# Attention kernel: the context copied out of its bank by ScalarE, the inverted row sums spread into their own bank, and new hand-written orders

## The reference

```python
qn  = layer_norm(x, q_norm_g, q_norm_b);  kvn = layer_norm(context, kv_norm_g, kv_norm_b)
Q, K, V = heads(qn @ Wq), heads(kvn @ Wk), heads(kvn @ Wv)
attn = softmax(Q @ K.T / sqrt(32))
ctx  = merge_heads(attn @ V)
out  = x + gelu(ctx @ Wo + bo)            # exact gelu
```

## Time and profile before

| what | value |
|---|---|
| median of 2 runs | 3285.81 us (3284.95 to 3286.67) |
| profiled execution, its own time | 3289.35 us |
| its span | 3287.5 us |
| PE busy | 3251.8 us, 99% of the span |
| DVE, ACT, POOL busy | 2255.8, 2278.0, 2314.0 us (69, 69, 70%) |
| DMA engines | about 60% busy |
| TensorE clock granted, mean | 0.995 |

### The profile page before, as it was taken

One profiled execution on the slowest core, in us unless ns is written; L12 is line 12 of the kernel. 1 busy time (PEld: TensorE's weight loads), 2 busy tenths in 40 slices (PEclk: granted clock), 3 DMA queues, 4 the chain that ended last, 5 costly groups with the idle time before them and its releaser, 6 DMA issues.

```text
span 3287.5 us, 60427 instructions
## 1 busy us (share of the span) xinstructions
PE 3251.8 (99%) x16611; PEld 2140.6 (65%) x16611; DVE 2255.8 (69%) x4775; ACT 2278.0 (69%) x3986; POOL 2314.0 (70%) x1543
## 2 busy tenths in 40 slices
PE   8999999999999999999999999999999999999998
PEld 5566666666666666666666666666666666666664
DVE  6677676776676676667766766766677667667664
ACT  4677767776667777677667667776776676677765
POOL 2677677777767776776777677767767766777765
PEclk9999999999999999999999999999999999999999
DMA  6566556566566666565665566665656655666653
GB/s 141 76 111 106 104 103 115 90 108 109 104 107 96 109 104 105 103 117 86 109 108 105 105 97 109 106 103 103 120 83 111 106 105 105 99 110 107 102 77 74
DMA packets 186492, 340.15 MB, mean 103 GB/s; under 512 B 20561, under 2 KB 20577, under 8 KB 186466
## 3 DMA queue, kind: packets, MB, share of 16 engines
q1 hardware_dynamic: 186000, 339.03, 60.0%
q10 hardware_dynamic: 466, 0.80, 0.2%
HBM read 104.87 MB, written 33.55 MB: 42 GB/s over the span
## 4 chain that ended last, share of the span: by engine, by line
PE 97%; DVE 1%; issue 1%; ACT 1%; DMA 0%; POOL 0%; SPq 0%; ACTq 0%; POOLq 0%; DVEq 0%
PE gen L820 42%; PE score L847 15%; PE score L840 15%; PE ctx L864 14%; PE gen L876 4%; PE gen L910 4%; PE gen L930 1%; DVE maxes L684 0%; POOL probs L463 0%; DMA k_stack<-k_nat 0%; PE score L766 0%; ACT q_stack L598 0%; PE ctx L795 0%; DVE stats L703 0%; PE gen L809 0%
## 5 line engine op out<-in xcount | busy, mean ns | idle before, releaser
L463 POOL TENSOR_TENSOR probs<-probs 128x1024 f32<-128x1024 f32 x762 | 1803.0, 2397 | 290.6 <-PE ctx L864 284.6
L684 DVE TENSOR_REDUCE maxes<-score 128x1 f32<-128x512 f32 x2048 | 1295.3, 681 | 199.9 <-PE score L847 199.0
L546 ACT ACTIVATE probs<-score 128x512 f32<-128x512 f32 x2048 | 1086.3, 620 | 141.3 <-PE score L840 136.2
L847 PE MATMUL score<-k_stack,q_stack 96*128 96x512 f32 x2048 | 761.2, 413 | 3.2 <-DVE maxes L684 2.2
L840 PE MATMUL score<-q_stack,k_stack 128*128 128x512 f32 x2048 | 698.1, 407 | 6.4 <-ACT q_stack L598 6.3
L847 PEld LDWEIGHTS score<-k_stack,q_stack 96*128 96x128 f32 x2048 | 378.5, 189 | 217.1 <-ACT probs L546 82.9
L840 PEld LDWEIGHTS score<-q_stack,k_stack 128*128 128x128 f32 x2048 | 374.1, 189 | 202.4 <-DVE maxes L684 58.2
L864 PE MATMUL ctx<-probs,v_sb 128*32 128x512 f32 x4096 | 492.5, 598 | 1.1 <-DVE ctx_n L700 1.1
L820 PE MATMUL gen<-w_v,cT 128*128 128x512 f32 x1536 | 462.2, 395 | 0.0
L820 PE MATMUL gen<-cT,w_k 128*128 128x512 f32 x1536 | 460.0, 398 | 0.2 <-DVE q_nat L666 0.2
L820 PE MATMUL gen<-xT,w_q 128*128 128x512 f32 x1536 | 450.5, 396 | 3.4 <-DVE w_q L622 0.4
(11 more groups left out here) (88 smaller groups left out, 2748.2 us busy)
## 6 DMA issues: line engine op xcount, KB each, us to landing
k_stack<-k_nat SPq DMA_DIRECT2D x384, 256.0 KB, 8.4
q_stack<-q_nat SPq DMA_DIRECT2D x381, 256.0 KB, 5.6
tok<-in_x SPq DMA_DIRECT2D x132, 256.0 KB, 10.4
tok<-in_ctx SPq DMA_DIRECT2D x128, 256.0 KB, 11.0
res<-in_x SPq DMA_DIRECT2D x124, 256.0 KB, 2.7
out<-res SPq DMA_DIRECT2D x124, 256.0 KB, 2.1
probs<-in_L_xattn_Wq SPq DMA_DIRECT2D x1, 1024.0 KB, 7.6
probs<-in_L_xattn_Wk SPq DMA_DIRECT2D x1, 1024.0 KB, 9.9
```

Of the source, the lines that this page charges most:

```text
L463: pool.tensor_tensor(probs[:, c + 1, heads], probs[:, c + 1, heads], probs[:, c, heads], ALU.add).then_inc(pool_added, 1)
L546: act.activation(probs[:, n, part, :], score_at(s, "st", i)[:], ACT.Exp, scale=SCALE).then_inc(exp_done, 1)
L684: dve.tensor_reduce(maxes[:, u1 % 2, SROW + i:SROW + i + 1], score_at(s, "s", i)[:], AX_X, ALU.max, negate=True).then_inc(max_done, 1)
L847: pe.matmul(score_bank(pe, b, s, "s", i)[:, :], q_stack[0:KROWS, u1 % 2, n, P * part:P * (part + 1)], k_stack[0:KROWS, u1 % 2, n, :], star ...
```

## The change

ACT gets a new instruction in each step, `cc`: it copies `ctx_ps` to a new tile `ctx_raw` in SBUF once the second `pv` is done, and it is now this copy that raises `ctx_read`. DVE's `zb` writes the spread inverses to the gen bank from which `zt` read the sums, instead of to `ctx_n`; `cn` multiplies `ctx_raw` by that bank and it is now `cn` that releases the gen bank (`free["z"]`). The space for `ctx_raw` comes from smaller tiles (`ones` has 32 columns, `max_hl` shares `max_cut`, some constants share a tile, the norm rows are loaded into `max_cut` before the first batch). The order of all five engines is new; the number of items of each kind over a batch is the same, apart from `cc`.

```diff
 OVER_BATCH = ("v", "o", "gelu", "res_add", "store", "res", "load", "ln", "la", "lv", "norm", "x", "first_res", "ob")
 ORDER = {
     "pe": (
-        "q*3 v q*2 v q v st*2 v*2 s st v s st s v*2 st s st s z v st*3 s v*2 st*2 s st k v s*4 pv st s st*2 o s "
-        "st s k s*2 pv m k o*2 k o k*2",
-        "o st*2 o st*3 q st q*4 st q st*3 z x k*3 x st*2 x st k*2 s k st s st*2 pv s x s x s x s pv s x s*2 o*3 "
-        "s*2 x o s o*2 s o s o*2 s o s o*3 m",
-        "o*4 s o s k s k s st k s st z st s st s q st q st s st*2 k st*3 k s st k st*4 pv s*2 q s q s*2 q s*2 q "
-        "pv m",
-        "k q k v q v k*2 st*3 k st*2 q st*2 k q st q st q st*2 z st*4 v st v s*3 pv s*2 v s*2 v s*2 v s v s*2 v*2 "
-        "s*2 v s*2 v pv m",
+        "q*3 v q*2 v q v st v st*3 v*2 s v s st*2 v s st*2 v z s k s st k s pv st v s st v s*2 v st s st k s st s "
+        "st*2 s*4 pv m o*3 k*3",
+        "o*2 st*2 o st*3 q st q st*3 q*2 st q*2 st x z st k*6 s x st x st*3 pv s x s x s x s*3 pv x o*2 s x o s o "
+        "s o s*2 o*4 s*2 o s*2 o*4 m",
+        "o*2 s*2 k o*2 k s*3 st k s q st k s q st*2 s st k st*4 z st*2 s*2 q st*3 k s st*2 pv s*2 q s*2 q*2 s pv "
+        "m",
+        "k q*2 k q k v k st*2 v st k st*2 q k st v st q st*3 q st*2 z st s st v st s st s pv s*3 v*2 s v s*2 v "
+        "s*2 v s*2 v s v*2 s*2 pv m",
     ),
     "act": (
-        "q st*4 v st*8 norm v split norm*2 st*4 mh mx*4 k",
-        "st*6 gelu q st x st*2 norm st*4 x k st*2 norm x norm st x*2 norm x norm x*2 gelu mh gelu mx*4 split",
-        "gelu st*12 k split st*4 q mh mx*4",
-        "st*6 k st*5 q st*4 split st v*2 mh mx*4",
+        "q st*2 cc st*2 v st*4 norm st norm*2 st split st v st*5 mh mx*4 k",
+        "st*8 gelu q cc x st*2 norm st*2 norm x k st x st*2 norm st x norm*2 x*4 gelu mh gelu mx*4 split",
+        "gelu st*2 cc st*11 k st*3 q mh split mx*4",
+        "st cc st*4 k st*5 q st*6 v split v mh mx*4",
     ),
     "dve": (
-        "q s ln s*2 la ln lv s ln s la*2 zt s zr lv zb s cn ln lv s la s*3 lv s*5 md ml ln*2 k ob",
-        "ln la*2 q zt lv*2 x la zr ln zb cn lv s la x k lv s x s*2 x*2 s*2 x s*3 x s*2 x s ob s*4 md ob ml",
-        "s ob s*6 zt s zr zb cn s k s*7 md q ml",
-        "k zt zr zb cn q s*16 md ml",
+        "q ln s*2 ln s la ln la lv*2 la ln s zt ln lv zr s zb cn la s*2 la s*3 lv s*6 md ml ln k ob",
+        "la ln la lv*2 q x zt zr ln zb cn lv s x la k x lv s*4 x*2 s x s x s*2 x s*2 ob s*5 md ob ml",
+        "s*2 ob s*6 zt zr s*2 k s zb cn s*5 md q ml",
+        "k zt s zr q s zb s cn s*13 md ml",
     ),
     "pool": (
-        "ln*3 split add*6 res_add ln*3",
-        "ln*2 add*5 res_add add res_add split res_add",
-        "split add*6",
+        "ln*3 add ln split add*5 res_add ln",
+        "ln*3 add*4 res_add add res_add add split",
+        "res_add add*6 split",
         "add split add*5",
     ),
     "sp": (
-        "load*8 rq rk store res",
-        "rq rk store res store",
-        "store first_res rk rq first_res",
+        "load*8 rq rk store",
         "rq rk",
+        "res store res store*2 rk rq first_res",
+        "first_res rq rk",
     ),
 }
 
...
+        ctx_raw = sb("ctx_raw", [P, D])
...
-        ones = sb("ones", [P, P])
+        ones = sb("ones", [P, DH])
...
+                        if kind == "cc" and valid(bp):
+                            wait(act, pv_done, 4 * (NU * bp + up) + 4)
+                            wait(act, free["z"], NU * bp + up)
+                            act.activation(ctx_raw[:], ctx_ps[:], ACT.Identity).then_inc(ctx_read, 1)
                         if kind == "split" and valid(bp):
-                            wait(act, ctx_read, NU * bp + up + 1)
+                            wait(act, free["z"], NU * bp + up + 1)
...
                             wait(dve, full["z"], tp + 1)
                             wait(dve, ctx_split, tp)
-                            dve.transpose(ctx_n[:], gen_at("z", up)[:]).then_inc(free["z"], 1)
+                            dve.transpose(ctx_n[:], gen_at("z", up)[:]).then_inc(z_turned, 1)
                         if kind == "zr" and valid(bp):
-                            wait(dve, free["z"], tp + 1)
+                            wait(dve, z_turned, tp + 1)
                             dve.reciprocal(z_inv[:], ctx_n[:].rearrange("p (b c) -> p b c", c=DH)[:, :, 0]).then_inc(z_inverted, 1)
                         if kind == "zb" and valid(bp):
                             wait(dve, z_inverted, tp + 1)
-                            dve.transpose(ctx_n[:].rearrange("p (b c) -> p b c", c=DH),
+                            dve.transpose(gen_at("z", up)[:].rearrange("p (b c) -> p b c", c=DH),
                                           z_inv[:].unsqueeze(2).to_broadcast([P, NZ, DH])).then_inc(z_spread, 1)
                         if kind == "cn" and valid(bp):
                             wait(dve, z_spread, tp + 1)
-                            wait(dve, pv_done, 4 * tp + 4)
-                            dve.tensor_tensor(ctx_n[:], ctx_ps[:], ctx_n[:], ALU.mult).then_inc(ctx_read, 1)
+                            wait(dve, ctx_read, tp + 1)
+                            dve.tensor_tensor(ctx_n[:], ctx_raw[:], gen_at("z", up)[:], ALU.mult).then_inc(free["z"], 1)
```

More of the change, by code:

```diff
@@ L201, in build @@
         ident = sb("ident", [P, P])
-        ones = sb("ones", [P, P])
+        ones = sb("ones", [P, DH])
         maxes = sb("maxes", [P, 2, P])
         max_cut = sb("max_cut", [P, P], F32R)
-        max_hl = sb("max_hl", [P, P], F32R)
-        cut_sign = sb("cut_sign", [P, 1])
-        low_row = sb("low_row", [P, 1])
+        row_consts = sb("row_consts", [P, 3])
+        cut_sign, low_row, minus_half = (row_consts[:, n:n + 1] for n in range(3))
         chunk_mask = sb("chunk_mask", [P, NC])
@@ L216, in build @@
         rstd = sb("rstd", [P, 8])
-        minus_half = sb("minus_half", [P, 1])
-        bias_q = sb("bias_q", [P, NU])
-        bias_k = sb("bias_k", [P, NU])
-        bias_v = sb("bias_v", [P, NU])
-        norm_rows = sb("norm_rows", [4 * NC, P])
+        bias_qkv = sb("bias_qkv", [P, 3, NU])
+        bias_q, bias_k, bias_v = (bias_qkv[:, n, :] for n in range(3))
         norm_cols = sb("norm_cols", [P, 4, NC])
@@ L652, in prepare @@
                     dve.wait_ge(bias_mm, 3)
[L653 removed]
+                    dve.tensor_copy(bias_v, score[3][:, 0:NU]).then_inc(bias_cols, 1)
                     low_weights(2, "v", 2)
@@ L759, in _ @@
             pe.wait_ge(cols_loaded, 16 * 4)
-            pe.matmul(score[3][:, 0:4 * NC], norm_rows[:], ident[0:4 * NC, 0:4 * NC], start=True, stop=True,
+            pe.matmul(score[3][:, 0:4 * NC], raw(max_cut[0:4 * NC, :]), ident[0:4 * NC, 0:4 * NC], start=True, stop=True,
                       is_transpose=True).then_inc(cols_mm, 1)
```

26 lines of the change are left out of this document (13 added, 13 removed).

## The result

| | before | after |
|---|---|---|
| median of 2 runs | 3285.81 us | 3348.64 us (3347.84 to 3349.45) |
| profiled execution, its own time | 3289.35 us | 3347.84 us |
| span | 3287.5 us | 3346.0 us |

The ratio is 1.0191 with a 95% interval of 1.0147 to 1.0235: the kernel became 63 us slower, and the interval leaves open whether that is more or less than 2%. The forecast was 3298 us, with a range up to 3322: the sum had 12 of the 63 us.

The account below looks back on a forecast made before the run. PE was taken as the bound, losing about 0.5 us per pass to waits. Terms of +0.25, +0.1, +0.1, 0 and -0.05 gave +0.4 us per pass, times 31 +12 us: median 3298 us, range 3262 to 3322.

Parts of the forecast that it names:

- the sum: All terms of one pass added: +0.4 us per pass, times 31, +12 us.
- The frame: Whole kernel: PE is the full engine at full clock, every product stays, and waits cost it about 0.5 us per pass.
- The copy's price: ACT's `cc`, four times a pass: 0.5 us each, costing nothing under 29.6 us of idle time; without cover 62 us.
- Step 0: Scores packed before the second `pv`: the last two wait for banks, 0.1 us per pass, at most 0.35.
- The bank of K in step 1: K's product takes Q's gen bank and waits for DVE's `q`: 0.25 us per pass, bounds 0.0 and 0.7.
- The bank held until `cn`: Gen bank released later: hidden in steps 0, 2 and 3; in step 1 the second `x` waits 0.1 us.
- Step 2: `cc` behind two exponentials delays those behind it by 0.5 us: costed at 0, from -0.3 to +0.3.
- Step 3: `pv` no longer waits for `cn`, behind which DVE idled 0.54 us: gain 0.05 us per pass, at most 0.5.
- The transposition at twice its price: Rival: `zb` into PSUM costs double, on PE's path in steps 1 and 3, 1.4 us per pass: 3341 us, chance 0.08.
- ACT becomes the bound in step 1: Rival: lateness at K passes through every score bank to the step's end, 1 us per pass more: 3329 us, chance 0.1.
- The rival that the new orders win: New orders win half to all of 0.6 us per pass: 3276 us, at the limit 3255; chance 0.3.
- ACT's two unknowns: Score waits in step 0, 0.1 us with bound 0.35, and exponentials delayed by `cc` in step 2, 0 within 0.3.

## Why the prediction was wrong, step by step

**The frame held.** The same products in the same count; full clock; PE sets the end; the loss is 1.90 us in each pass. But the sum had +0.4.

**The copy's price was right and its cover was not: the main error, 28 us.** "It costs nothing as long as that idle time covers it" took the idle time of a pass, 29.6 us, for cover of an instruction at a certain place. The term in the sum was 0; the runs with full and one-column copies measured 0.92 us a pass for its length. `cc` stands between exponentials (at 1559.01 in step 2, and so in step 0), each of which frees a score bank that PE comes for. The timeline of ACT in step 0:

```profile
1499.82 1.28 ACT L544 ACTIVATE probs<-score 128x512 f32<-128x512 f32 x2
1500.99 0.59 ACT L549 ACTIVATE ctx_raw<-ctx 128x512 f32<-128x512 f32 x1
1501.47 1.09 ACT L544 ACTIVATE probs<-score 128x512 f32<-128x512 f32 x2
```

Everything behind the copy is 0.48 us later until ACT idles next. In step 0 that costs PE nothing, in steps 1 to 3 it does. The prediction itself counted this delay in step 1 for `x` ("`cc` more"), and for step 2 ("delays those behind it by 0.5 us"), and still set the latter at 0.

**Step 0 was mis-sized nearly eightfold, 24 us.** The sum had 0.1, its bound 0.35, the runs 0.77 us a pass. The method was right, scores of 0.23 against slots of 0.5, but it let only the last two of the twelve scores wait. The fifth weight load is the first late one, and in the pass shown four of the last eight wait. How much of it is ACT's and how much DVE's no run takes apart, and the run with the old step 0 changes the orders of PE, ACT, DVE and POOL there together.

**The bank of K in step 1: 0.25 predicted, at most 0.1 found.** K's first weight load stands idle for 0.10 us there, and no longer wait shows. Another bank was later. After the new order it is `z` that takes the bank of the output product before it, which `gelu` releases; in the old order `x`, one product later, took it. The timeline of PE, then of ACT:

```profile
1528.10 0.60 PE L912 MATMUL gen<-ident,tok 128*128 128x128 f32 x4
1528.88 1.06 PE L878 MATMUL gen<-probs,ones 128*32 128x512 f32 x8 [0.18 <-ACT act_out L565]
```

```profile
1526.85 1.28 ACT L565 ACT_TABLE_LOAD   x1
1528.15 0.60 ACT L565 ACTIVATE act_out<-gen 128x512 f32<-128x512 f32 x1
```

`z` starts 0.78 us after the transpose ahead of it, where 0.35 is the distance. I had moved `gelu` by two exponentials in the working for K, and didn't ask who else waits for it.

**The bank held until `cn`: right.** Predicted 0.1 us at the second `x` of step 1, found 0.08; in the other steps nothing. The run of the structure in old orders shows that this is the doing of the new order: there the same hold costs 133 us, a good fifth of it by the lower clock behind the wait. The prediction said that holding the bank longer has a price in one step of four. That is so in both orders, and it is the order of that step which makes it 0.08 or 4.3 us a pass.

**Step 2 was put at 0 and cost 0.5.** 0.63 more up to `z`, 0.15 less behind it. Half of the 0.63 is the copy (0.33 with one column). And one wait more, at the end of the step: K's first product of step 3 takes the bank of Q, since `z` and `q` changed places, and DVE's remainder of Q stands behind the maxima of step 2. DVE, then PE:

```profile
1572.01 0.17 DVE L745 TENSOR_REDUCE maxes<-maxes 128x16 f32<-128x16 f32 x1
1572.10 0.74 DVE L668 SCALAR_TENSOR_TENSOR q_nat<-gen,bias_qkv,q_nat 128x512 fp32r<-128x512 f32 x1
```

```profile
1572.53 0.33 PE L932 MATMUL gen<-ident,maxes 128*128 128x128 f32 x1
1572.90 0.74 PE L822 MATMUL gen<-cT,w_k 128*128 128x512 f32 x2
```

`q_nat` is done at 1572.84, and K starts at 1572.90, 0.37 us behind `m`; in the kernel before the product there starts 0.08 us behind it. The prediction looked at the bank of Q in step 1 only.

**Step 3: the reason was false, the number nearly right.** `pv` never waited for `cn` in a way that counts. The idle 0.54 us of DVE was read as PE being held, from a row that shows only that no score came; PE was at work on `pv`. The new step 3 does win, 8 us; the runs changed PE's, ACT's and DVE's order of that step together, so which of them wins is not shown.

**The rivals.** The transposition at twice its price is out (712 ns). "ACT becomes the bound in step 1", 3329 us at a chance of 0.1, was the nearest: the lateness of ACT was indeed passed on through the score banks, but in all four steps and not in step 1 alone. Its argument against, that ACT has idle time and later work, is the error named first. The rival that the new orders win has its grain of truth in step 3.

**The range** stopped at 3322 because the bounds of ACT's two unknowns were taken from two scores in step 0 and from ±0.3 in step 2, and the copy had no upper bound but the whole of it, 62 us, which I left out. With half of that added it would have reached 3353.

**What stays open.** The copy and step 0 account for 52 of the 63 us. The last 11 lie by the lost times at `gelu`'s bank, at K behind Q's remainder and in the scores ahead of `z` in step 2, less what step 3 wins. The two runs that took one of these away moved the wait without removing it, so their single prices are argued and not shown.

## What to carry to other kernels

An engine's idle time covers an added instruction only at the place where it lies: list who is released by each instruction behind it, up to the engine's next idle stretch, and put a copy that is not urgent into such a stretch (here behind the last exponentials of a step, the copy's length cost 3 us in place of 28 and 33). Where a producer is twice as fast as what empties its banks, count the whole run of such tiles against the banks, not its last ones. When the order of products over a ring of banks changes, write out anew for each product whose bank it takes and what frees it.

## What the runs showed of the hardware

- A vector product with both inputs in SBUF took 2.78 us when POOL's addition, which reads SBUF, had started 0.17 us before; with one input in PSUM, at the same offset, 0.69 us. Started clear of it or ahead of it, the SBUF form took 0.67 to 0.69 us as well.
- A weight load that comes late can cost more than it waits. In a stream the load runs 0.22 us ahead of its matmul, and matmuls start 0.23 us apart. In the kernel after, where PE's weight load had stood idle for 0.25 us or more ahead of a score, the matmul started with its load and the next one 0.34 us later (as from 1513.75 to 1514.09). At idle times of 0.15 to 0.2 us the next one came, on the mean, 0.25 us later in the kernel before and 0.29 in the kernel after. By this the eleven waits more in each pass come to 1.2 us at most behind them, beside the waits themselves.
- Where PE had stood idle for 3.2 us, in the new structure with the old orders, the granted clock was 0.50 (1.2 GHz) behind it, and a transpose and the start of the next score were 0.76 us apart instead of 0.35. The wait cost about 3.4 us and this 0.9 us more.
